# A double-buffered, reordered scan in the receptance stage of a macaron RWKV layer

## The reference, cut to what matters

```python
xk = hidden * time_mix_key + shifted * (1.0 - time_mix_key)      # xv and xr alike
k = jnp.einsum('bsh,dh->bsd', xk, Wk)
v = jnp.einsum('bsh,dh->bsd', xv, Wv)
r = jax.nn.sigmoid(jnp.einsum('bsh,dh->bsd', xr, Wr))
rwkv = _wkv_scan(time_decay, time_first, k, v)
return jnp.einsum('bsd,hd->bsh', r * rwkv, Wo)
# _wkv_scan, one step (w = -exp(time_decay), without the running maximum):
#   out = (num + exp(k + time_first) * v) / (den + exp(k + time_first))
#   num = exp(w) * num + exp(k) * v ;  den = exp(w) * den + exp(k)
```

## Time and profile before

| | us |
|---|---|
| two runs | 9829.02 and 10351.44, median 10090.23 |
| the profiled execution, its own time | 9825.84 |
| its span on the slowest core (core 1) | 9824.3 |
| spans of the eight cores | 9797.2 to 9824.3 |
| receptance stage with the scan, in it | 5292 to 6150 |

### The profile page before, as it was taken

The page is one execution under the profiler, slowest core; times in us unless marked ns, Lnnn a source line. Parts: engine busy times, 40 slices in busy tenths (PEclk is TensorE's granted clock), DMA queues, the critical chain, the costliest instruction groups (busy, mean ns, idle before and its releaser), DMA issues.

```text
span 9824.3 us, 84601 instructions; the slowest of 8 cores (9797.2 to 9824.3 us)
## 1 busy us (share of the span) xinstructions
PE 6939.2 (71%) x31729; PEld 3202.0 (33%) x31729; DVE 3954.0 (40%) x3971; ACT 1043.0 (11%) x1062; POOL 164.1 (2%) x72
## 2 busy tenths in 40 slices
PE   0021999999971288882666331844999999978888
PEld 0010444444430033330322110321444444433333
DVE  0036555555546533335443444245222222253333
ACT  5541000000000000001001222010000000000000
POOL 0000000000000000000000121000000000000000
PEclk9965999999985599995877766956999999989999
DMA  8974333333327766665333111742212212146666
GB/s 293 314 264 179 144 150 138 140 142 147 137 95 229 245 208 208 210 214 182 143 133 116 75 75 66 228 151 96 76 69 75 72 69 78 69 148 219 204 209 196
DMA packets 390255, 1524.19 MB, mean 155 GB/s; under 512 B 41285, under 2 KB 74454, under 8 KB 289494
## 3 DMA queue, kind: packets, MB, share of 16 engines
q1 hardware_dynamic: 232282, 1183.13, 35.9%
q10 hardware_dynamic: 152832, 318.83, 8.7%
q0 software_dynamic: 4736, 16.81, 0.4%
HBM read 1183.03 MB, written 335.58 MB: 155 GB/s over the span
## 4 chain that ended last, share of the span: by engine, by line
PE 61%; DVE 18%; DMA 14%; ACT 4%; issue 2%; POOL 1%; ACTq 1%; DVEq 0%; SPq 0%; POOLq 0%
PE pb L595 18%; PE pb L602 18%; PE pb L721 14%; PE pb L1034 5%; DMA wbuf<-wgu 4%; DVE tmp L768 3%; PE pb L529 2%; DMA terndn<-tern 2%; PE pb L1128 2%; DMA wbuf<-wdn 2%; DMA gsb<-g1d 2%; DMA wbuf<-wr 1%; ACT wbuf L308 1%; DVE tmp L772 1%; DVE bfA L775 1%
## 5 line engine op out<-in xcount | busy, mean ns | idle before, releaser
L721 PE MATMUL pb<-bfA,tern 128*128 128x512 bf16 x7936 | 1806.8, 390 | 284.1 <-DVE bfA L775 277.9
L595 PE MATMUL pb<-bfA,tern 128*128 128x512 bf16 x8192 | 1855.9, 380 | 9.1 <-DVE tern L562 9.1
L602 PE MATMUL pb<-bfA,tern 128*128 128x512 bf16 x8192 | 1851.6, 379 | 0.0
L1034 PE MATMUL pb<-bfA,tern 128*128 128x512 bf16 x3072 | 699.2, 392 | 791.5 <-DVE tern L919 791.5
L721 PEld LDWEIGHTS pb<-bfA,tern 128*128 128x128 bf16 x7936 | 787.1, 100 | 1305.3 <-issue 439.1
L602 PEld LDWEIGHTS pb<-bfA,tern 128*128 128x128 bf16 x8192 | 801.5, 98 | 966.6
L595 PEld LDWEIGHTS pb<-bfA,tern 128*128 128x128 bf16 x8192 | 802.4, 98 | 867.3 <-issue 17.7
L536 DVE TENSOR_REDUCE macc<-pb 128x4 f32<-128x512 f32 x512 | 354.8, 693 | 1693.1 <-PE pb L529 1662.2
L1034 PEld LDWEIGHTS pb<-bfA,tern 128*128 128x128 bf16 x3072 | 307.4, 100 | 1184.3 <-issue 844.9
L617 ACT ACTIVATE tmp<-tmp 128x512 f32<-128x512 f32 x512 | 322.8, 630 | 3448.8 <-DVE tmp L612 3448.8
L740 DVE TENSOR_TENSOR tmp<-pb,bcst 128x512 f32<-128x512 f32 x128 | 88.6, 692 | 1230.6 <-PE pb L721 1217.6
(11 more groups left out here) (119 smaller groups left out, 3482.1 us busy)
## 6 DMA issues: line engine op xcount, KB each, us to landing
tern<-terndn SPq DMA_DIRECT2D x496, 512.0 KB, 4.1
wbuf<-wgu SPq DMA_DIRECT2D x64, 2048.0 KB, 11.2
wbuf<-wdn SPq DMA_DIRECT2D x128, 1024.0 KB, 7.1
wbuf<-wgu SPq DMA_DIRECT2D x128, 1024.0 KB, 10.0
g1d<-gsb ACTq DMA_DIRECT2D x512, 256.0 KB, 2.6
gsb<-g1d SPq DMA_DIRECT2D x128, 1024.0 KB, 6.0
terngu<-tern ACTq DMA_DIRECT2D x128, 512.0 KB, 8.5
tern<-terngu SPq DMA_DIRECT2D x128, 512.0 KB, 4.3
```

Of the source, the lines that this page charges most:

```text
L595: p.op("tensor", lambda e, g=g, t=t, tt=ta, ba=ba: e.matmul(out=pb[ba][:], lhsT=TT(tt)[:, g * 128:(g + 1) * 128], rhs=AR(g)[:, t * 512:(t ...
L602: p.op("tensor", lambda e, g=g, t=t, tt=tb_, bb=bb: e.matmul(out=pb[bb][:], lhsT=TT(tt)[:, g * 128:(g + 1) * 128], rhs=AR(g)[:, t * 512:(t ...
L721: bb=bk: e.matmul(out=pb[bb + l][:], lhsT=TT(sl)[:, ko * 512 + l * 128: ko * 512 + (l + 1) * 128], rhs=AR512(og), start=(og == 0), stop=(o ...
L1034: p.op("tensor", lambda e, g=g, t=t, wsl=wsl, b=b: e.matmul(out=pb[b][:], lhsT=TT(wsl)[:, g * 128:(g + 1) * 128], rhs=AR(g)[:, t * 512:(t ...
```

## The change

Exp(k) and v get two buffers each, taken in turn; the second pair lies in `rows`. The loads of group dg wait for group dg-2 instead of dg-1, and use a semaphore of their own for each parity. av moves from `emit_scan` to the end of `emit_scan_loads`, that is in GpSimd's queue behind bv of the group before; it waits for its loads and for the numerator scans of the group before (av still has one buffer). ew waits for the denominator scans of the group before instead of for all of it. den is written ahead of num on VectorE, and Ln waits for den alone. The store to `zd` is issued by ScalarE, behind Exp and ahead of the sigmoids, instead of by GpSimd, and has a semaphore for each parity. The order of the stages, all shapes and the arithmetic stay.

```diff
--- before.py
+++ after.py
-            st_a, st_v, st_av = WS(3), GS(1), GS(0)
-            st_b, st_bv = st_a, WS(2)
+            ST_A = (WS(3), rows[:, 0:2048])
+            ST_V = (GS(1), rows[:, 2048:4096])
+            st_av, st_bv = GS(0), WS(2)
...
             def emit_scan_loads(dg):
-                p.wait("sync", "DV", scan_it_dv.get(dg - 1, 0))
-                p.wait("sync", "AC", scan_ac.get(dg - 1, 0))
-                p.wait("sync", "PL", scan_pl.get(dg - 1, 0))
-                p.wait("sync", "LS0", p.cnt["LS0"])
-                p.dma("sync", "LS0", lambda e, dg=dg: e.dma_start(
-                    out=st_a, in_=kvsp[dg]))
-                p.wait("sync", "LS1", p.cnt["LS1"])
-                p.dma("sync", "LS1", lambda e, dg=dg: e.dma_start(
-                    out=st_v, in_=vsp[dg]))
+                par = dg % 2
+                sa, sv = (f"LS{par * 2}", f"LS{par * 2 + 1}")
+                p.wait("sync", "DV", scan_it_dv.get(dg - 2, 0))
+                p.wait("sync", "AC", scan_ac.get(dg - 2, 0))
+                p.wait("sync", "PL", scan_pl_bv.get(dg - 2, 0))
+                p.wait("sync", sa, p.cnt[sa])
+                p.dma("sync", sa, lambda e, dg=dg, par=par: e.dma_start(
+                    out=ST_A[par], in_=kvsp[dg]))
+                p.wait("sync", sv, p.cnt[sv])
+                p.dma("sync", sv, lambda e, dg=dg, par=par: e.dma_start(
+                    out=ST_V[par], in_=vsp[dg]))
+                p.wait("gpsimd", sa, p.cnt[sa])
+                p.wait("gpsimd", sv, p.cnt[sv])
+                p.wait("gpsimd", "DV", scan_nacc_dv.get(dg - 1, 0))
+                p.op("gpsimd", lambda e, par=par: e.tensor_tensor(
+                    out=st_av, in0=ST_A[par], in1=ST_V[par], op=ALU.mult))
+                scan_pl_av[dg] = p.cnt["PL"]
...
             def emit_scan(dg):
-                p.wait("scalar", "DV", scan_it_dv.get(dg - 1, 0))
+                par = dg % 2
+                sa, sv = (f"LS{par * 2}", f"LS{par * 2 + 1}")
+                st_a, st_v = ST_A[par], ST_V[par]
+                st_b = st_a
+                p.wait("scalar", "DV", scan_dacc_dv.get(dg - 1, 0))
                 p.op("scalar", lambda e, dg=dg: e.activation(
                     out=t_ew, in_=tmp[:, 0:1024], func=AF.Identity, scale=0.0,
                     bias=cols[:, CEW + dg:CEW + dg + 1]))
-                p.wait("gpsimd", "LS0", p.cnt["LS0"])
-                p.wait("gpsimd", "LS1", p.cnt["LS1"])
-                p.wait("gpsimd", "DV", scan_it_dv.get(dg - 1, 0))
-                p.op("gpsimd", lambda e: e.tensor_tensor(
-                    out=st_av, in0=st_a, in1=st_v, op=ALU.mult))
-                pl_av = p.cnt["PL"]
-                p.wait("vector", "AC", p.cnt["AC"])
-                p.wait("vector", "PL", pl_av)
-                p.wait("vector", "LS0", p.cnt["LS0"])
+                ew_ac = p.cnt["AC"]
+                p.wait("vector", "AC", ew_ac)
+                p.wait("vector", "PL", scan_pl_av[dg])
...
-                dv_dacc = p.cnt["DV"]
-                p.wait("scalar", "DV", dv_dacc)
-                p.wait("scalar", "PL", pl_av)
-                p.op("scalar", lambda e, dg=dg: e.activation(
+                scan_dacc_dv[dg] = p.cnt["DV"]
+                p.wait("scalar", "DV", scan_dacc_dv[dg])
+                p.wait("scalar", "PL", scan_pl_av[dg])
+                p.op("scalar", lambda e, dg=dg, st_b=st_b, st_a=st_a: e.activation(
                     out=st_b, in_=st_a, func=AF.Identity,
                     scale=cols[:, 112 + dg:112 + dg + 1]))
                 scan_ac[dg] = p.cnt["AC"]
-                p.wait("gpsimd", "AC", p.cnt["AC"])
-                p.op("gpsimd", lambda e: e.tensor_tensor(
+                p.wait("gpsimd", "AC", scan_ac[dg])
+                p.wait("gpsimd", "DV", scan_num_dv.get(dg - 1, 0))
+                p.op("gpsimd", lambda e, st_b=st_b, st_v=st_v: e.tensor_tensor(
                     out=st_bv, in0=st_b, in1=st_v, op=ALU.mult))
-                scan_pl[dg] = p.cnt["PL"]
-                p.wait("vector", "PL", p.cnt["PL"])
+                scan_pl_bv[dg] = p.cnt["PL"]
+                p.wait("vector", "AC", scan_ac[dg])
+                p.op("vector", lambda e, st_b=st_b: e.tensor_tensor(
+                    out=t_den2[:, 1:2048], in0=t_dacc2[:, 0:2047],
+                    in1=st_b[:, 1:2048], op=ALU.add))
+                p.op("vector", lambda e, st_b=st_b: e.tensor_copy(
+                    out=t_den2[:, 0:1], in_=st_b[:, 0:1]))
+                den_dv = p.cnt["DV"]
+                p.wait("vector", "PL", scan_pl_bv[dg])
                 p.op("vector", lambda e: e.tensor_tensor(
                     out=t_num2[:, 1:2048], in0=t_nacc2[:, 0:2047],
                     in1=st_bv[:, 1:2048], op=ALU.add))
                 p.op("vector", lambda e: e.tensor_copy(
                     out=t_num2[:, 0:1], in_=st_bv[:, 0:1]))
-                p.wait("vector", "AC", scan_ac[dg])
-                p.op("vector", lambda e: e.tensor_tensor(
-                    out=t_den2[:, 1:2048], in0=t_dacc2[:, 0:2047],
-                    in1=st_b[:, 1:2048], op=ALU.add))
-                p.op("vector", lambda e: e.tensor_copy(
-                    out=t_den2[:, 0:1], in_=st_b[:, 0:1]))
-                p.wait("scalar", "DV", p.cnt["DV"])
+                scan_num_dv[dg] = p.cnt["DV"]
+                p.wait("scalar", "DV", den_dv)
                 p.op("scalar", lambda e: e.activation(out=t_rec2, in_=t_den2,
                                                       func=AF.Ln))
                 p.op("scalar", lambda e: e.activation(out=t_rec2, in_=t_rec2,
                                                       func=AF.Exp, scale=-1.0))
-                p.wait("vector", "AC", p.cnt["AC"])
+                rec_ac = p.cnt["AC"]
+                p.wait("vector", "AC", rec_ac)
                 p.op("vector", lambda e: e.tensor_tensor(
                     out=t_wkv2, in0=t_num2, in1=t_rec2, op=ALU.mult))
-                rqs = 2 + dg % 2
-                p.wait("vector", "TZ", rq_tz.get(dg - 2, 0))
+                rqs = 2 + par
+                if dg < 2:
+                    p.wait("vector", f"LT{rqs}", p.cnt[f"LT{rqs}"])
+                p.wait("vector", f"TR{par}", rq_tr.get(dg - 2, 0))
                 p.op("vector", lambda e, rqs=rqs: e.tensor_tensor(
                     out=TT(rqs), in0=t_wkv2, in1=tmp[:], op=ALU.mult))
-                scan_it_dv[dg * 2 + 1] = p.cnt["DV"]
                 scan_it_dv[dg] = p.cnt["DV"]
-                p.wait("gpsimd", "DV", p.cnt["DV"])
-                p.wait("gpsimd", "LT2", p.cnt["LT2"])
-                p.wait("gpsimd", "LT3", p.cnt["LT3"])
-                p.wait("gpsimd", "TZ", rq_tz.get(dg - 1, 0))
-                p.dma("gpsimd", "TZ", lambda e, dg=dg, rqs=rqs: e.dma_start(
+                p.wait("scalar", "DV", scan_it_dv[dg])
+                p.wait("scalar", f"TR{par}", p.cnt[f"TR{par}"])
+                p.dma("scalar", f"TR{par}", lambda e, dg=dg, rqs=rqs: e.dma_start(
                     out=zd[dg], in_=TT(rqs)))
-                rq_tz[dg] = p.cnt["TZ"]
+                rq_tr[dg] = p.cnt[f"TR{par}"]
...
-                        p.wait("scalar", "DV", scan_it_dv.get(dc * 2 - 1, 0))
+                        p.wait("scalar", "DV", scan_it_dv.get(dc - 1, 0))
```

More of the change, by code:

```diff
@@ L932, in proj_era @@
             scan_it_dv = {}
+            scan_nacc_dv = {}
+            scan_dacc_dv = {}
+            scan_num_dv = {}
             scan_ac = {}
-            scan_pl = {}
-            rq_tz = {}
+            scan_pl_bv = {}
+            scan_pl_av = {}
+            rq_tr = {}
             def emit_scan_loads(dg):
-                p.wait("sync", "DV", scan_it_dv.get(dg - 1, 0))
-                p.wait("sync", "AC", scan_ac.get(dg - 1, 0))
-                p.wait("sync", "PL", scan_pl.get(dg - 1, 0))
-                p.wait("sync", "LS0", p.cnt["LS0"])
-                p.dma("sync", "LS0", lambda e, dg=dg: e.dma_start(
-                    out=st_a, in_=kvsp[dg]))
-                p.wait("sync", "LS1", p.cnt["LS1"])
-                p.dma("sync", "LS1", lambda e, dg=dg: e.dma_start(
-                    out=st_v, in_=vsp[dg]))
-            def emit_scan(dg):
-                p.wait("scalar", "DV", scan_it_dv.get(dg - 1, 0))
+                par = dg % 2
[15 more added lines that the diff above has]
+                scan_pl_av[dg] = p.cnt["PL"]
+            def emit_scan(dg):
+                par = dg % 2
[3 more added lines that the diff above has]
+                p.wait("scalar", "DV", scan_dacc_dv.get(dg - 1, 0))
                 p.op("scalar", lambda e, dg=dg: e.activation(
@@ L967, in emit_scan @@
                     initial=t_nacc2[:, 1023:1024], op0=ALU.mult, op1=ALU.add))
-                p.op("vector", lambda e: e.tensor_tensor_scan(
+                scan_nacc_dv[dg] = p.cnt["DV"]
+                p.wait("vector", sa, p.cnt[sa])
+                p.op("vector", lambda e, st_a=st_a: e.tensor_tensor_scan(
```

(10 more changed lines are left out.)

## The result

| | before | after |
|---|---|---|
| median of all runs | 10331.16 us (10 runs) | 10025.58 us (13 runs) |
| lowest | 9829.02 us | 9650.63 us |
| from first scan to last product, core 5 | 748.1 us | 575.4 us |
| the same over the eight cores | 741.0 to 748.1 us, median 742.5 | 575.3 to 575.6 us |

The account below looks back on a forecast made before the run. No engine fills the receptance stage; a serial chain does, 44.1% of a period put down to a weight transfer. Groups of 30.77, 14 x 36.84 and 32.34 us total 578.9 against 742.65: 9825.84 - 163.8 = 9662 us, range 9560 to 9725.

Parts of the forecast that it names:

- The chain and its period: Receptance stage's scan groups: one step after another, period falling from 47.37 to 36.84 us, sixteen groups 578.9 against 742.65.
- Prefetching: Loads issued a group ahead: the 12.04 us before the cast are hidden by the whole group before.
- the order of den: VectorE, den ahead of num: Ln no longer waits for bv and num; den starts at 18.05 us, beside bv.
- Taking turns: VectorE two-input operations beside GpSimd products: the later waits until the earlier is done, giving the 36.84 us period.
- Rival B: Two-input VectorE operations do not wait for GpSimd; period 30.79 us, 256 less, 9570 us; chance 0.22.
- C: They wait, but GpSimd's av starts only when VectorE finishes the group; period 32.34, 231 less, 9594 us; chance 0.10.
- D: GpSimd keeps its turn: bv, then av, and den waits for both; period 39.95, 114 less, 9712 us; chance 0.10.
- E: Slower: products of VectorE and GpSimd stretch beside each other; 10.5 us more a group loses the gain; chance 0.03.
- F: No prefetch: a wait left in SP's queue ends with the group before; 87 us less, 9739 us; chance 0.05.
- The store: Result's store issued by ScalarE ahead of the sigmoids: 0.43 us a group, bounds nothing and 0.59.
- the starting term of the sum: Time of the profiled execution before, 9825.84 us, set with the lower of two runs, 9829.02 and 10351.44.
- The case I gave 0.63: Whole kernel: the measurement lies within about 2% (196.5 us) of no change; chance 0.63.

Follow-up runs that it names:

- e1: Changed kernel, with av of the next group waiting for the last VectorE product instead of the numerator scans; 9601.93 us, period 32.3.
- e3: Changed kernel, with the loads of a group waiting for the group just before it again; 9741.0 us, period 40.8.
- e4: Changed kernel, with num written ahead of den again on VectorE and Ln waiting for both; 9766.91 us, period 42.3.
- e5: Changed kernel, with num replaced by a one-input VectorE sum over column pairs and wkv reading bv (output wrong on purpose); lowest 9628.3 us, period 33.9.
- e2: Changed kernel, with the store of the result back in GpSimd's queue between bv and the next av; 9612.23 us, period 32.3.
- e7: Changed kernel with b, bv folded into VectorE's den, num; av on VectorE, sigmoids behind Exp, store in SP's queue; ratio to kernel before 0.9708, lowest 9542.96 us.
- e10: The kernel of e8 timed a second time, unchanged; lowest 9464.85 us against 9822.3 for the kernel before, 0.964.
- e8: Kernel of e7 with only the store moved from SP's queue to GpSimd's; lowest 9466.63 us against 9825.79 for the kernel before, period 24.0.

## Why the prediction was right and where it was not

**The chain and its period: right.** The period was forecast at 36.84 us and is mostly 36.55 on core 5; the sixteen groups took 575.4 us against 578.9 worked out. Scans at 5.99 after the product (6.07), the end of b at 17.79 (17.88), den at 17.96 (18.05), bv to 24.61 (24.84), num and its copy to 31.7 (32.05). The 0.3 between the two periods is the sum of these tenths, and the last distance is 32.19 where 32.34 was worked out. Prefetching and the order of den, undone one at a time, give 4.5 and 6.0 us of the 11.0 by which the average fell. One reading in the prediction is off without changing the sum: the second held cast stands four groups on from the first (5682.65 against 5492.57), not six.

**Taking turns: right, and shown for two inputs.** The trace of before had only a cast held by GpSimd; extending it to operations with two inputs was the decision on which the sum stood. The runs show it: num is 2.29 us in e1 and e3, with av elsewhere, and 6.6 in e4, with av beside it again. In e5 the sum over pairs, with one input, is not held, but the one-input cast is, so what makes an operation one that is held stays open beyond these kinds. Rival B (30.8) is out. C (32.3) is out as to who goes first, since av takes its turn 0.03 us ahead of num; but its period is what e1 and e2 reach by keeping av away. D is out: den gets in before bv, by 0.09 us. E is out: the two engines' products take turns and do not stretch, since num ends 2.15 us after av and av keeps its 4.50. F is out: no cast waits for a weight. The Trainium skill, "SBUF — State Buffer", section "Who interferes with whom", has a VectorE instruction with two SBUF inputs contend with a GpSimd one that reads SBUF, and the later of the two wait; 6.62 against 2.29 us for num and 6.56 against 4.49 for bv agree, in both directions.

**The store: right in size** (the table load starts 0.55 us after the last product instead of 0.13, which is 0.42 for the 0.43 taken), **but one effect of it was passed over.** I costed the move by its issue time on ScalarE and didn't say what its leaving did to GpSimd's queue: as long as the store stood there, av could not start before the last product. e2 shows that to be worth 4.0 us a group, some ten times the issue time: the sum had av beside num, and did not say that this came from moving the store.

**The time of the whole: wrong, through the term that the sum starts from.** The measured median of 10025.58 us lies outside my range of 9560 to 9725. The step that failed is the starting term of the sum, 9825.84, together with the one sentence on how it stands to the runs shown: I had two runs, 9829.02 and 10351.44, set the sum against the lower, and built the range from the unknown costs of the change alone. The median of ten runs of the kernel before is 10331.16, so that term was 505.3 us too low for a median, more than three times the forecast change. Seven of the ten runs before lie 427 to 623 us above the lowest, and nine of the thirteen after 331 to 900 us; the range had no room for either. Against the lowest time, 9650.63, the sum of 9662 fits. The difference of medians, 305.6 us, is no measure of the change. The lowest times differ by 178.4, and the stretch that the sum worked out fell by 167 (median of the eight cores) beside the 163.8 forecast, so the terms of the change itself held.

**Size against the 2%.** 163.8 us were 1.67%; the ratio says 2.05% with 1.4 to 2.7 as interval. The case I gave 0.63, between the bounds, is neither shown nor excluded by it.

## What to carry to other kernels

When work of two engines is moved side by side, ask what both read: here a VectorE operation with two SBUF inputs, or the cast of the weight, and a GpSimd product came out one after the other, so GpSimd work paid only where VectorE had nothing of that kind, under ScalarE's sigmoids. An instruction that waits for the end of an iteration holds all that stands behind it in its queue: that was the weight load's trouble before and again in e7, and in e2 it was what kept the two engines apart. Moving one such instruction has to be read on the queue it leaves as well as on the one it enters.

## What the runs showed of the hardware that was not expected

- The one-column copy between num and wkv is not held by av (0.15 us at 5530.69 in e5, in the middle of av), though the 2048-column cast is the earlier trace rows.
- Beside a cast it is GpSimd that comes out longer when it starts second: av 5.49 us for 4.5 (e1), and a store's issue 0.85 for 0.59, ending 0.12 us after the cast in e2 and 0.11 in the rows of e10.
- Where the granted clock of an execution is lower, the scan stretch is not where it is lost. The stretch takes 575.3 to 575.6 us on all eight cores of the changed kernel's profile, though the whole execution is granted 0.84 on cores 0 to 3 and 0.87 on cores 4 to 7; within the stretch it is 0.70 on core 0 and 0.71 on core 5. In the kernel of e8 and e10 the period is 24.0 us on core 5 of e8 (0.81 over the execution, 0.79 in the stretch) and on core 0 of e10 (0.87 and 0.78). What the stretch would take at a clock that is lower within it, no run shows.
